# Nine layers whose output products, residual and normalising become one stage that works tile by tile

## The reference

```
h = layernorm(x, eps=1e-5)
x = x + layer(h) @ W_o + b_o
```

## Time and profile before

| | us |
|---|---|
| median of 3 runs | 2666.93 (2666.87 to 2674.51) |
| profiled execution | 2669.26 |
| its span | 2667.4 |
| busy: PE / DVE / ACT / POOL | 2354.3 / 1460.5 / 1055.5 / 381.9 |
| mean granted TensorE clock | 0.921 of 2.4 GHz |

### The profile page before, as it was taken

The page is one execution under the profiler, slowest core; times in us unless marked ns, Lnnn a source line. Parts: engine busy times, 40 slices in busy tenths (PEclk is TensorE's granted clock), DMA queues, the critical chain, the costliest instruction groups (busy, mean ns, idle before and its releaser), DMA issues. The chain is left out here.

```text
span 2667.4 us, 38992 instructions
## 1 busy us (share of the span) xinstructions
PE 2354.3 (88%) x15232; PEld 1367.6 (51%) x15232; DVE 1460.5 (55%) x2285; ACT 1055.5 (40%) x1896; POOL 381.9 (14%) x659
## 2 busy tenths in 40 slices
PE   2899999988999998999997687886879999988778
PEld 1344444435699663454453444352238657464547
DVE  4777877623222456888884685226976332323333
ACT  2466666612111233777774372124422233120310
POOL 2454000000000400000001250002630000000000
PEclk8799999998999997999999768987999999888789
DMA  7977553120554699456430001001025240101100
GB/s 197 234 186 166 103 114 57 26 99 2 228 204 175 167 302 236 93 93 133 93 60 35 12 1 61 29 1 65 0 91 178 95 174 0 52 1 51 54 0 8
DMA packets 108359, 258.62 MB, mean 97 GB/s; under 512 B 11824, under 2 KB 83088, under 8 KB 94224
## 3 DMA queue, kind: packets, MB, share of 16 engines
q1 hardware_dynamic: 104144, 213.73, 30.1%
q0 software_dynamic: 2736, 39.37, 4.4%
q10 hardware_dynamic: 1296, 3.03, 0.3%
HBM read 211.26 MB, written 44.83 MB: 96 GB/s over the span
## 5 line engine op out<-in xcount | busy, mean ns | idle before, releaser
L704 DVE TENSOR_REDUCE sta_parts<-sta_psA 128x1 f32<-128x1024 f32 x544 | 626.0, 1188 | 187.4 <-PE sta_psA L621 185.7
L762 ACT ACTIVATE sta_probs<-sta_psS 128x512 f32<-128x512 f32 x1056 | 575.8, 596 | 274.1 <-PE sta_psS L632 272.2
L632 PE MATMUL sta_psS<-L_xattn_qS,L_xattn_kst 99*128 99x256 bf16 x2112 | 356.1, 278 | 11.3 <-ACT sta_probs L762 6.6
L621 PE MATMUL sta_psA<-L_xattn_kst,L_xattn_qS 99*128 99x512 bf16 x1088 | 293.3, 387 | 46.5 <-PEq L59 32.0
L632 PEld LDWEIGHTS sta_psS<-L_xattn_qS,L_xattn_kst 99*128 99x128 bf16 x2112 | 161.6, 98 | 258.8 <-ACT sta_probs L762 183.2
L641 PE MATMUL sta_psO<-sta_probs,L_xattna_V 128*32 128x256 f32 x2560 | 189.5, 385 | 0.0
L621 PEld LDWEIGHTS sta_psA<-L_xattn_kst,L_xattn_qS 99*128 99x128 bf16 x1088 | 104.3, 99 | 131.3 <-DVE sta_parts L704 43.5
L235 ACT ACT_TABLE_LOAD x14 | 18.0, 1283 | 262.1 <-PEq L59 262.1
L1046 ACT ACTIVATE sht_probs<-sht_psS 128x768 f32<-128x768 f32 (+1 forms) x64 | 55.3, 864 | 151.5 <-PE sht_psS L890 100.0
L641 PE MATMUL sta_psO<-sta_probs,L_xattn_V 128*32 128x256 f32 x1536 | 114.8, 390 | 0.0
L481 POOL CAST sta_split<-sta_neg 128x2 bf16<-128x2 f32 x64 | 12.2, 190 | 715.4 <-issue 467.4
(11 more groups left out here) (631 smaller groups left out, 4012.3 us busy)
## 6 DMA issues: line engine op xcount, KB each, us to landing
L_xattn_kst<-L_xattn_keys SPq DMA_DIRECT2D x186, 136.0 KB, 5.0
L_xattn_kst<-L_xattn_keys SPq DMA_DIRECT2D x186, 128.0 KB, 4.7
L_xattn_values<-prj_rows SPq DMA_DIRECT2D x64, 256.0 KB, 3.8
L_xattn_keys<-prj_parts SPq DMA_DIRECT2D x32, 384.0 KB, 4.0
L_xattna_V<-in_ctxV SPq DMA_DIRECT2D x5, 2048.0 KB, 11.7
L_xattna_V<-L_xattn_values SPq DMA_DIRECT2D x5, 2048.0 KB, 10.7
l2f_W<-in_M SPq DMA_DIRECT2D x10, 1024.0 KB, 8.8
L_xattn_keys<-sta_bparts SPq DMA_DIRECT2D x24, 384.0 KB, 7.1
```

The source lines that it names most:

```text
L621: last = nc.tensor.matmul(psA[:, u % 2, col:col + rhs.shape[1]], lhsT, rhs, start=True, stop=True)
L632: last = nc.tensor.matmul(psS[:, at % 2, j * T:(j + 1) * T], lhsT, rhs, start=True, stop=True)
L704: nc.vector.tensor_reduce(into(parts[:, u // n % 2]), view(psA[:, u % 2, :]), AX.X, ALU.max).then_inc(max_taken, 1)
L762: nc.scalar.activation(probs[:, u % NP, i * 512:(i + 1) * 512], psS[:, at % 2, :], ACT.Exp, scale=scale).then_inc(probs_ready, 1)
```

## The change

A new stage `residual_rows` does for a seam what the last `gemms` and `normalize` did. TensorE makes product 0, then in turn product t and the transposes of tile t - 1, six fillers, the transposes of the last tile, and six fillers. VectorE does for each tile: the add to X, bn_stats, bn_aggr, variance, (ScalarE: root), reciprocal, normalising, each waiting for the one before. Three transposed tiles are copied by ScalarE, the last by VectorE. The ten fillers at the start of `normalize` are gone from the nine seams. The bias of five output products is no product any more: VectorE adds it to the whole of X at the stage's start, and the bias is stored on all partitions. `xn` and `xnT` are now two tiles shared by all layers. Prefetches that `normalize` started are started by the new stage or by the next `gemms`; the waits for loaded weights move into the new stage. The cast of `lines` moves into the new stage of L0_xattn, the four memsets of L1_attn into its first `gemms`. `first_loads` of L3_attn grow from 1024 to 2048 columns. Five calls of `normalize` stay (L0_xattn, L1_xattn, L3_xattn twice, L3_attn) and the one at the end of L3_ffn.

```diff
+def residual_rows(nc, K, X, products, update, xn, xnT, eps, bias=None, weight=None, begin=(), await_loads=False, cast=None):
...
+            @block.sync
+            def _(sp):
+                K["weight_loads"].start(sp, begin)
+                if await_loads:
+                    K["weight_loads"].wait(sp)
+
+            @block.gpsimd
+            def _(gp):
+                if cast:
+                    K["weight_loads"].wait(gp)
+                    cast().then_inc(cast_done, 1)
+                    gp.wait_ge(cast_done, 1)
+
+            @block.tensor
+            def _(pe):
+                def make(t):
+                    for i, term in enumerate(products[t]):
+                        last = nc.tensor.matmul(banks[:, t, 0:C], *term, start=i == 0, stop=i == len(products[t]) - 1)
+                    last.then_inc(product_ready, 1)
+
+                def turn(t):
+                    pe.wait_ge(rows_ready, t + 1)
+                    for k in range(KC):
+                        dst = psT[:, k, t * P:(t + 1) * P] if t < NT - 1 else psL[:, k, :]
+                        last = nc.tensor.transpose(dst, xn[:, t, k * P:(k + 1) * P], K["ident"])
+                    if t >= NT - 2:
+                        last.then_inc(turned, 1)
+
+                def fill():
+                    for _ in range(6):
+                        nc.tensor.matmul(psI[:], K["ident16"], K["mask16_q"], start=True, stop=True)
+
+                make(0)
+                for t in range(1, NT):
+                    make(t)
+                    turn(t - 1)
+                fill()
+                turn(NT - 1)
+                fill()
+
+            @block.vector
+            def _(dve):
+                step = Steps(dve, dve_step)
+                V = nc.vector
+                if bias is not None:
+                    step(add_bias(nc, X, bias))
+                for t in range(NT):
+                    dve.wait_ge(product_ready, t + 1)
+                    step(update(t, banks[:, t, 0:C], step))
+                    step(V.bn_stats(stats[:, t, :], X[:, t, :]))
+                    step(V.bn_aggr(mv[:, t, :], stats[:, t, :]))
+                    mean, one = mv[:, t, 0:1], rstd[:, t:t + 1]
+                    if weight is None:
+                        V.tensor_scalar(var[:, t:t + 1], mv[:, t, 1:2], eps, None, ALU.add).then_inc(var_ready, 1)
+                    else:
+                        step(V.tensor_tensor(square[:, t:t + 1], mean, mean, ALU.mult))
+                        step(V.tensor_tensor(square[:, t:t + 1], square[:, t:t + 1], mv[:, t, 1:2], ALU.add))
+                        V.tensor_scalar(var[:, t:t + 1], square[:, t:t + 1], eps, None, ALU.add).then_inc(var_ready, 1)
+                    dve.wait_ge(sd_ready, t + 1)
+                    step(V.reciprocal(one, sd[:, t:t + 1]))
+                    if weight is None:
+                        V.tensor_scalar(xn[:, t, :], X[:, t, :], mean, one, ALU.subtract, ALU.mult).then_inc(rows_ready, 1)
+                    else:
+                        step(V.tensor_scalar(xn[:, t, :], X[:, t, :], one, None, ALU.mult))
+                        V.tensor_tensor(xn[:, t, :], xn[:, t, :], weight[:, :], ALU.mult).then_inc(rows_ready, 1)
+                dve.wait_ge(turned, 2)
+                V.tensor_copy(xnT[:, :, rest], psL[:]).then_inc(stored, 1)
+
+            @block.scalar
+            def _(act):
+                nc.scalar.activation(sd[:, NT:NT + 1], K["ones"][:, 0:1], ACT.Sqrt)
+                for t in range(NT):
+                    act.wait_ge(var_ready, t + 1)
+                    nc.scalar.activation(sd[:, t:t + 1], var[:, t:t + 1], ACT.Sqrt).then_inc(sd_ready, 1)
+                act.wait_ge(turned, 1)
+                for k in range(KC):
+                    nc.scalar.copy(xnT[:, k, first], psT[:, k, first]).then_inc(stored, 1)
...
-def add_to_residual(nc, K, X, W, attT, kc, bias, begin=()):
-
-    gemms(nc, K, project_rows(W, C, attT, lambda t: vadd(nc, X[:, t, :], X[:, t, :]), "v",
-                           bias=bias, kc=kc, ones=K["ones"][0:1, :]), begin=begin)
+def add_bias(nc, X, bias):
+
+    return nc.vector.tensor_tensor(X[:], X[:], bias.unsqueeze(1).to_broadcast([P, NT, C]), ALU.add)
+
+
+def output_rows(nc, K, X, W, attT, kc, bias=None, **more):
+
+    residual_rows(nc, K, X, [[(attT[:, k, t * P:(t + 1) * P], W[:, k, 0:C]) for k in range(kc)] for t in range(NT)],
+                  lambda t, ps, step: nc.vector.tensor_tensor(X[:, t, :], ps, X[:, t, :], ALU.add), K["xn"], K["xnT"], 1e-5, bias, **more)
...
-        normalize(nc, K, X, xn, xnT, 1e-5, begin=K["begin"]["L1_xattn"])
-        gemms(nc, K, project_rows(w["gate"], E, xnT, lambda t: vcopy(nc, logits[:, t, :]), "v"))
+        gemms(nc, K, project_rows(w["gate"], E, xnT, lambda t: vcopy(nc, logits[:, t, :]), "v"), begin=K["begin"]["L1_xattn"])
...
-             "L2_xattn": weights("L2_xattn", 197.25), "L3_xattn": weights("L3_xattn", 183.5), "L3_attn": weights("L3_attn", 163.5, 1024),
+             "L2_xattn": weights("L2_xattn", 197.25), "L3_xattn": weights("L3_xattn", 183.5), "L3_attn": weights("L3_attn", 163.5, 2048),
```

More of the change, by code:

```diff
@@ L189, in _ @@
                     K["weight_loads"].wait(sp)
[L191 to L198, removed]
             @block.vector
@@ L252, in _ @@
                     nc.tensor.matmul(psI[:], K["ident16"], K["mask16_q"], start=True, stop=True)
-def gemms(nc, K, jobs, ring=4, loads=(), vector=(), scalar=(), await_loads=None, begin=()):
+def residual_rows(nc, K, X, products, update, xn, xnT, eps, bias=None, weight=None, begin=(), await_loads=False, cast=None):
+    with pool(nc, f"fin{nc.next_id()}") as p:
+        stats = p.sb("stats", [P, NT, 6])
+        mv = p.sb("mv", [P, NT, 2])
+        var = p.sb("var", [P, NT])
+        sd = p.sb("sd", [P, NT + 1])
+        rstd = p.sb("rstd", [P, NT])
+        square = p.sb("square", [P, NT])
+        banks = p.ps("banks", [P, NT, 512])
+        psT = p.ps("psT", [P, KC, 512])
+        psL = p.ps("psL", [P, KC, P])
+        psI = p.ps("psI", [P, 512])
+        first = slice(0, (NT - 1) * P)
+        rest = slice((NT - 1) * P, NTOK)
+        with stage(nc, "product_ready", "dve_step", "var_ready", "sd_ready", "rows_ready", "turned", "stored", "cast_done") as \
+                (block, product_ready, dve_step, var_ready, sd_ready, rows_ready, turned, stored, cast_done):
+            @block.sync
[68 more added lines that the diff above has]
+                    nc.scalar.copy(xnT[:, k, first], psT[:, k, first]).then_inc(stored, 1)
@@ L262, in gemms @@
+def gemms(nc, K, jobs, ring=4, loads=(), vector=(), scalar=(), await_loads=None, begin=(), pool_engine=()):
     with pool(nc, f"gem{nc.next_id()}") as p:
@@ L270, in view, with _ @@
                 return banks[0:jobs[n][0], n % ring, 0:jobs[n][1]]
+            @block.gpsimd
+            def _(gp):
+                step = Steps(gp, pool_step)
+                for one in pool_engine:
+                    step(one())
             @block.sync
@@ L1352, in cross_attention @@
                            key_loads, value_loads, blocks, lambda i: i // 8 * 8)
-        add_to_residual(nc, K, X, w["o"], attT, 4, w["bo"], begin=K["begin"]["L0_attn" if raw else "L1_attn"])
+        if raw:
+            output_rows(nc, K, X, w["o"], attT, 4, w["bo"], begin=K["begin"]["L0_attn"], await_loads=True,
+                        cast=lambda: nc.gpsimd.tensor_copy(K["lines"], K["ahead"]["L0_attn"]["lines"]))
+        else:
+            output_rows(nc, K, X, w["o"], attT, 4, w["bo"], begin=K["begin"]["L1_attn"], await_loads=True)
 def lora_attention(nc, K, X, arrays, specs, own, ahead):
+    xnT = K["xnT"]
     with pool(nc, "l2x") as p:
-        xn = p.sb("xn", [P, NT, C])
-        xnT = p.sb("xnT", [P, KC, NTOK])
         side = K["ahead"]["L2_side"]
@@ L1796, in hyperbolic_attention @@
             rows = {n: p1.sb(f"R_{n}", [P, NT, 512]) for n in NAMES}
-            normalize(nc, K, X, xn, xnT, 1e-5, await_loads=True, pool_engine=[lambda n=n: nc.gpsimd.memset(rows[n][:], 0.0) for n in NAMES])
             ones = K["ones"][0:1, :]
@@ L1805, in hyperbolic_attention @@
                           lambda: nc.scalar.activation(soft[:], soft[:], ACT.Ln, bias=K["ones"][:, 0:1]),
-                          lambda: nc.scalar.activation(safe[:], w["qk_scale"], ACT.Sigmoid)])
+                          lambda: nc.scalar.activation(safe[:], w["qk_scale"], ACT.Sigmoid)],
+                  pool_engine=[lambda n=n: nc.gpsimd.memset(rows[n][:], 0.0) for n in NAMES])
             def heads(n):
@@ L2726, in rope_and_groups @@
             short_attention(nc, K, q, k, v, attT, 0.25, False, 32, we.loads)
[L2727 to L2728 removed]
+            residual_rows(nc, K, s1, [[(attT[:, k, t * P:(t + 1) * P], w["o"][:, k, 0:C]) for k in range(4)] for t in range(NT)],
+                          lambda t, ps, step: nc.vector.tensor_tensor(s1[:, t, :], ps, xn[:, t, :], ALU.add), x1, x1T, 1e-6, weight=w["norm1_w"])
         acc = p.sb("acc", [P, NT, C])
```

93 lines of the change are left out of this document (39 added, 54 removed).

## The result

| | before | after |
|---|---|---|
| median, us | 2667.93 (4 runs, 2666.87 to 2674.51) | 2646.17 (4 runs, 2645.93 to 2647.15) |
| ratio | | 0.9909, 95% interval 0.9894 to 0.9925 |
| profiled execution, us | 2669.26 | 2646.34 |
| its span, us | 2667.4 | 2644.5 |
| mean granted clock | 0.921 | 0.92 |

What follows compares the result with a forecast made beforehand. Nine barrier-separated seams, serial chains with nothing beside them, were on the path: 134.3 us, 5% of the span. Seam gains less losses summed to 20.9, say 21 us, off 2669.26: 2648, or 2646 on the median's scale; range 2637 to 2658.

Steps and rivals of the forecast that it cites:

- The new stage of 11.0 us: A warm seam of four-step products takes 11.0 us from first residual add to next stage; VectorE's chain 2.1 per tile.
- L1_xattn, the largest term: L1_xattn to L1_attn seam: memsets leave the normalisation, 20.47 + 0.63 - 11.0 = 10.1 us gained.
- The adds beside the memsets: L1_attn's first product stage: adds of PSUM products beside the moved memsets; between nothing and 1.8 us, taken as nothing.
- L0_attn's seam: L0_attn to L0_ffn: 16.35 + 1.2 for the slow bias, less 11.0 and 1.7 for a slow second product: 4.9 us gained.
- The clock in L1_ffn's seam: L1_ffn to L2_xattn: VectorE's pace loses 2.6 us; a clock fall could add up to 2.7, half taken: loses 4.0.
- The two gate stages: Gate products before L0_ffn's and L2_ffn's experts: SyncE's prefetch issues outlast them, costing 2.2 and 3.6 us.
- L2_xattn: L2_xattn to L2_attn: a fifth, low-rank step makes TensorE slower; window 11.7 us, gain 4.6.
- L3_attn: L3_attn to L3_ffn: eight-step products, TensorE sets the pace; window 15.2 us, gain 1.9.
- The cast: L0_xattn's joined stage: GpSimd's cast of `lines` can hold up VectorE's TENSOR_SCALAR, 0 to 1.45 us; 0.7 taken.
- C: Joined seams: each of a tile's seven instructions waits 0.08 us longer; 15 us lost, 2661; chance 0.18 with milder forms.
- D: Joined stages: TensorE's clock falls, a seam grows by 7 us; seven such seams lose 50, 2696; chance 0.05.
- B: Cheaper edges: L1_ffn's clock holds, 3.50 of issuing an accident, cast hits nothing, clock periods fall well: 2639; chance 0.15.

Runs made afterwards that it cites:

- the kernels with the short filler: The kernel after with one filler product instead of six after the joined stage's last transposes: 2635.91 us; with three other edits as well: 2633.86 us.
- the late prefetches: The kernel after with the two gate stages' prefetches issued by SyncE at the start of the experts' stages instead: 2643.41 us, ratio 0.9905.
- the kernels with the split seam: The kernel after with the L1_ffn seam alone made of two stages again, products then batched normalising: 2641.37 us, ratio 0.9908.
- the two combined ones: The kernel after with L1_ffn's seam in two stages, prefetches in the experts' stages, cast on ScalarE: 2642.89 us; with one last filler as well: 2633.86 us.

## Why the prediction came out, and where it did not
- **The new stage of 11.0 us.** Right. The three seams of warm four-step products whose stage no cast touches took 10.77, 10.78 and 10.86. Tiles follow at 2.17 on average in L1_xattn, close to the 2.1 of VectorE's chain.
- **L1_xattn, the largest term.** Right in size (10.3 for 10.1) and now taken apart: memsets 6.1, bias 2.1, joining 2.1. The adds beside the memsets in the new place cost nothing, as taken. Timeline of the kernel after:

```profile
1455.54 1.81 POOL L1897 MEMSET l1b_R_kE<- 128x2048 f32 x1
...
1456.85 0.69 DVE L420 TENSOR_TENSOR l1b_qk<-gem_banks,L_attn_weights 128x512 f32<-128x512 f32 x1 [1.03 <-PE gem_banks L387]
```

  A memset runs until 1457.35 over an add of 0.69 us, and the other three adds take 0.69 as well. The Trainium skill says on its page "SBUF — State Buffer" ("SBUF: two separate sides") that VectorE and GpSimd exclude each other only over a shared port pair; by that an add with one of its two operands in PSUM is not held up, and these rows agree.
- **L0_attn's seam.** Mis-sized: 6.3, not 4.9. I had put 1.7 for a slow second product, which would make the window 12.7; it took 11.12, only 0.3 over a warm one. The first product is at half clock before and after, but then the clock rises sooner: it is 0.94 in the window, for 0.88 before. It did so in every kernel with VectorE's bias (gains of 6.0 to 6.3, the kernels with the short filler apart), and not in the one with the bias product, whose window of this seam takes 14.14 us at 0.86. So the extra 1.4 goes with the removed one-row products; why the clock rises sooner without them no run tells.

```profile
654.89:669.03 14.14, 13.24 (x51) 8.17 (x51) 7.48 (x25) 1.55 (x6) 0.00 (x0) 0.86 0.00 1
```

- **The clock in L1_ffn's seam.** Mis-sized: the 2.6 of VectorE's pace was right to 0.1 (12.34 for 12.4), and the 1.4 on top never came: I had argued from the earlier trace rows that the clock could fall here, and it was 1.00 over the whole window; three more kernels that keep this stage as it is took 12.33 or 12.34 too. I had also read the earlier trace rows wrongly: its window of 3 us with 0.76 us of work lies behind the fall, since the clock is 0.50 in all of it. Ahead of the fall TensorE stood still for 2.24 us (from 1459.14 to 1461.38 in the kernel before) while the clock was still 1.00; in the joined stage of L1_ffn its longest idle time is 1.86. The Trainium skill's page "TensorE: Matmul & The Clock Gate" ("Part 4: PE-mode transpose") says that transposes don't count in the same way as TensorE being busy, and that spoke for the full 2.7. It was not borne out: the clock held, and the seam lost nothing beyond VectorE's pace.
- **The two gate stages.** The mechanism was right (SyncE's last issue ends them), and the late prefetches prove it. The first cost 1.6 for 2.2: its eight issues took 3.66 us, from 663.58 to 667.24, not the 4.3 of the earlier trace rows. The second cost 1.9 for 3.6, as the prediction had it for the case that the 3.50 us of issuing in the earlier trace rows was a single event. It was: here the same four issues took 1.76.

```profile
1965.32 1.76 SPq L1162 DMA_DIRECT2D L_xattn_weights<-in_L_xattn  x4
1967.12 2.14 SPq L1162 DMA_DIRECT2D L_context<-in_ctxQ  x4
```

- **L2_xattn.** Mis-sized by 0.5 us: 12.18, not 11.7. The five-step product and the turn make TensorE the slower engine, as the step had it, but its period is 2.7 us, in which VectorE waits 0.3 to 0.6 before each add; the three periods make 7.9 (1767.99 to 1775.91). The prediction gave its 11.7 without a sum; less the 2.2 of the last tile and the 2.1 behind it, it had left 7.4 for them.

```profile
1770.46 0.42 DVE L1486 TENSOR_TENSOR top_X<-fin_banks,top_X 128x256 f32<-128x256 f32 x1 [0.30 <-PE fin_banks L281]
...
1773.19 0.42 DVE L1486 TENSOR_TENSOR top_X<-fin_banks,top_X 128x256 f32<-128x256 f32 x1 [0.56 <-PE fin_banks L281]
...
1775.91 0.43 DVE L1486 TENSOR_TENSOR top_X<-fin_banks,top_X 128x256 f32<-128x256 f32 x1 [0.55 <-PE fin_banks L281]
```

- **L3_attn.** Its window was right (15.07 for 15.2). The gain of the whole stage was 0.3, since the first product took 5.41 us at a clock of 0.68, against 3.73 before at 1.00. In the kernels with the split seam, with the bias product and in the two combined ones it took 3.72 or 3.73, and in the first three of these the stage gained 2.0. The code of that product, which has no bias, is the same in all of them. So the 1.7 came or stayed away with the clock, and the 1.9 was right where it stayed away.

```profile
2383.09:2388.50 5.41, 5.41 (x17) 4.49 (x18) 0.00 (x0) 1.45 (x2) 0.00 (x0) 0.68 0.01 2
```

- **The cast** hit in full: 1.3 us for the 0.7 that I had taken between 0 and 1.45. The first loads of L3_attn cost nothing, as taken: its normalising stage took 5.99 us. **Not foreseen** was that L0_ffn's experts are 1.3 us longer. TensorE is busy there nearly all the time (209.1 of 210.2 us), and the length goes with the granted clock of the first 24 us (windows of the kernels before and after):

```profile
674.06:698.06 24.00, 23.39 (x75) 13.34 (x76) 6.74 (x29) 3.03 (x4) 3.16 (x4) 0.86 0.38 148
```

```profile
667.69:691.69 24.00, 23.38 (x72) 12.98 (x73) 6.61 (x29) 3.03 (x4) 0.81 (x2) 0.79 0.48 199
```

  With the memsets alone moved it is 0.86 again, and the stage takes 208.9 as before; with the late prefetches it is 0.79 and the stage takes 210.6; with the bias product 0.73 and 211.6. The late prefetches did bring the four one-row products at the start from 3.77 to 2.78 us (2.16 before), and the clock of the first 10 us from 0.50 to 0.66, but it is 0.88 in the next 14, for 1.00. What lowers the clock there stays open.

**The rivals.** C, a chain that waits 0.08 us more at each step, fell: the gaps are 0.03 to 0.04, as in the earlier trace rows. D, a clock that falls in the joined stages, fell: seven of the nine windows are at 0.97 or more, and the two at 0.94 took 12.21, with the cast in it, and 11.12. B was half true (the clock held, the issue was an accident; the cast hit after all). The profiled pair gained 22.9 us, the two medians are 21.8 apart, and the forecast gain was 20.9. That the median came within 0.2 us of 2646 is luck to the amount of some 2 us: the sum rests on errors against me (L0_xattn 0.7, L2_xattn 0.8, L3_attn 1.6, between the seams 0.8) and for me (L0_attn 1.4, L1_ffn 1.4, the gate stages 2.3, 0.5 in the rest).

## What to carry to other kernels
Joining a product stage and the reduction behind it tile by tile pays the pace of the slower engine once for each tile: work out both engines' period for one tile first, and leave apart those seams in which the vector chain is longer than the product that should hide it. Such a change brings other moves with it, and here these were together worth more than the joining: the bias off TensorE 10.7 us and the memsets off the normalisation 6.1, against 10.3 from joining less 3.5 for the prefetches that it pushed into two short stages. Try them by themselves. What ends a short stage is often not its arithmetic but what was hung onto it: DMA issues, filler products, a GpSimd operation over a normalisation; look at the last instruction of each engine before the barrier. Where one part is worth less than the total wanders between executions, measure it in its own window, not by the whole time.

## What the runs showed of the chip that I had not expected
- The same code of one layer takes 113.0 to 118.1 us with the granted clock (0.92 to 0.86), while the other engines' busy times stay equal; L1_attn's body 148.9 at 0.75 and 151.8 at 0.70. I found nothing in the edits that decides it.
- One GpSimd cast on 3 partitions, 1.45 us long, stretched a VectorE TENSOR_SCALAR on 128 partitions from 0.41 to 1.70 us when it began 0.10 after it, and left the two of its neighbours at 0.41 when it began at 553.22, between them.
- Fillers that stood at the end of each stage cost 0.8 us each time and bought no clock that shows in the seams or in the whole. One gate stage behind a seam had a lower clock without them (3.06 us for 2.45); whether they would hold it up each time is not shown.
